# Local attention layers of a two-layer block: opening norm in pairs of chunks, rotary sums by accumulating transfers, a stated program slot

## The reference

```
h = layernorm(x) * (1 + cb) + sb
for i in range(6):
    h = attn_layer(shift_tokens(h), ...) + h        # 16 heads of 64, windows of 32
    h = ffn_layer(shift_tokens(h), ...) + h
attn_layer: q = l2norm(q) * qs;  k = l2norm(k) * ksc
            q = q * cos * scale + rotate_half(q) * sin * scale
            k = k * cos / scale + rotate_half(k) * sin / scale
            softmax of a window's q against its own and the previous window's k, times v, times Wo
```

## Time and profile before

| | |
|---|---|
| median of 3 runs | 4979.4 us (4970.4 to 4989.2) |
| the profiled execution | 4985.0 us, its span 4983.1 us |
| busy in the span | TensorE 81%, VectorE 74%, ScalarE 63%, GpSimd 22% |
| DMA | 336.8 MB, 68 GB/s on average |

### The profile page before, as it was taken

How to read it: one execution, slowest core, us unless ns; L and a number is a source line. 1 busy time by engine, 2 the same in 40 slices (tenths; PEclk the granted TensorE clock), 3 DMA queues, 4 the chain that set the end, 5 groups by cost and what they waited for, 6 DMA issues and landing times. The chain is left out here.

```text
span 4983.1 us, 174228 instructions
## 1 busy us (share of the span) xinstructions
PE 4053.0 (81%) x68188; PEld 2876.0 (58%) x68188; DVE 3701.7 (74%) x6683; ACT 3147.4 (63%) x8447; POOL 1095.9 (22%) x856
## 2 busy tenths in 40 slices
PE   7947888888888888888888888888888888886578
PEld 4725566665666666665666656666666666654234
DVE  4837777777777877777777777787777777774765
ACT  4715766666666666766666667667766667663233
POOL 0002222222222222222222222222222222220112
PEclk9959999999999999999999999999999999997688
DMA  0012222222222222222222222222222222220000
GB/s 26 1 58 82 72 76 73 75 91 78 70 77 71 82 85 78 76 74 74 88 82 77 74 76 80 87 78 78 74 74 90 83 78 73 75 75 24 0 7 11
DMA packets 126167, 336.76 MB, mean 68 GB/s; under 512 B 32592, under 2 KB 33744, under 8 KB 125264
## 3 DMA queue, kind: packets, MB, share of 16 engines
q1 hardware_dynamic: 125520, 326.63, 20.4%
HBM read 22.41 MB, written 2.10 MB: 5 GB/s over the span
## 5 line engine op out<-in xcount | busy, mean ns | idle before, releaser
L1172 ACT ACTIVATE loc_probs<-loc_pair,loc_ebias,loc_rnorm 128x64 f32<-128x64 f32 x3072 | 1200.6, 433 | 10.9 <-DVE loc_ebias L1332 7.8
L873 POOL TENSOR_TENSOR loc_ks<-loc_mcos,loc_swapped 128x1024 f32<-128x1024 f32 x192 | 452.1, 2354 | 1776.6 <-DVE loc_kr L1320 1375.0
L920 PE MATMUL loc_pair<-loc_hs,loc_wqk 128*128 128x256 f32 x3072 | 751.4, 388 | 47.5 <-issue 43.1
L873 POOL TENSOR_TENSOR loc_qr<-loc_mcos,loc_swapped 128x1024 f32<-128x1024 f32 x192 | 452.2, 2355 | 1270.6 <-DMA loc_swapped<-loc_msin 1204.6
L1172 ACT ACTIVATION_READ_ACCUMULATOR loc_probs<-loc_pair,loc_ebias,loc_rnorm 128x1 f32 x3072 | 719.6, 234 | 0.0
L920 PEld LDWEIGHTS loc_pair<-loc_hs,loc_wqk 128*128 128x128 f32 x3072 | 568.0, 192 | 151.9 <-issue 64.4
L1330 DVE TENSOR_REDUCE loc_mx<-loc_pair 128x8 f32<-128x512 f32 x384 | 264.5, 689 | 410.1 <-PE loc_pair L964 402.9
L1272 DVE SCALAR_TENSOR_TENSOR loc_mcos<-loc_pair,loc_scal,loc_tab 128x1024 f32<-128x1024 f32 x384 | 490.5, 1277 | 86.7 <-ACT loc_sq L1154 65.3
L1154 ACT ACTIVATE loc_sq<-loc_pair 128x1024 f32<-128x1024 f32 x384 | 396.9, 1034 | 204.2 <-PE loc_pair L920 204.2
L1281 DVE SCALAR_TENSOR_TENSOR loc_msin<-loc_pair,loc_scal,loc_tab 128x1024 f32<-128x1024 f32 x384 | 489.6, 1275 | 9.1 <-DMA loc_swapped<-loc_msin 8.9
L964 PE MATMUL loc_pair<-loc_kr,loc_qr 64*32 64x64 f32 x24576 | 322.9, 226 | 122.0 <-issue 121.4
(11 more groups left out here) (228 smaller groups left out, 7457.6 us busy)
## 6 DMA issues: line engine op xcount, KB each, us to landing
loc_swapped<-loc_msin SPq DMA_DIRECT2D x768, 256.0 KB, 2.6
loc_veven<-loc_vodd SPq DMA_DIRECT2D x768, 64.0 KB, 2.2
loc_veven<-loc_vodd SPq DMA_DIRECT2D x384, 128.0 KB, 2.3
loc_wqk<-wqk_dram SPq DMA_DIRECT2D x12, 512.0 KB, 4.6
loc_wv<-wv_dram SPq DMA_DIRECT2D x6, 512.0 KB, 4.1
loc_wo<-wo_dram SPq DMA_DIRECT2D x6, 512.0 KB, 4.5
x<-xT_dram SPq DMA_DIRECT2D x1, 2048.0 KB, 7.4
loc_tab<-tables_dram SPq DMA_DIRECT2D x1, 2048.0 KB, 7.6
```

The lines of the kernel that those rows point to most:

```text
L873: nc.gpsimd.tensor_tensor(dst, mcos[i % 2][:, :], swapped[:, :], ALU.add).then_inc(rope_add, 1)
L920: ins = nc.tensor.matmul(pairs[b][:, p // 2, (p % 2) * UNIT:(p % 2 + 1) * UNIT], wqk[:, k, w:w + P], hs[u.odd][:, :], start=True, stop=True)
L1172: ins = nc.scalar.activation(probs[x][:, p, hp, :], pairs[b][:, hp, p * 2 * WIN:(p + 1) * 2 * WIN], ACT.Exp, bias=ebias[x][:, k:k + 1], sc ...
```

## The change

- The opening norm has two `LayerNorm` objects with buffers and banks of their own and one set of semaphores. Each phase is issued for both chunks of a pair before the next phase; TensorE's and VectorE's waits on `normed_ready` and `out_ready` go by pairs. The waits for the constants and the mask copies stand behind the loop.
- `mcos` and `swapped` are gone; `msin` and `ks` are double. `rotate_cos` writes into `ks` or `qr`, waiting for readers of two units before. GpSimd issues two transfers that add `msin`, even and odd partitions exchanged, to it. `rotated` and SyncE's `halves_across` are gone. `rotate_sin` waits for the transfer of the product two before; `scale_keys` and `scores` wait for two transfers each (`landed`). The `swap_ready` semaphores start at 0.
- TensorE's pipelined loop states `head_slot` 208: its first instruction is placed at slot 208 of a block of 256 program slots.

```diff
-    def tensor_mean(self, pe, n, src, wide):
+    def tensor_mean(self, pe, n, src, wide, before=None):
-        pe.wait_ge(self.normed_ready, START + n)
+        pe.wait_ge(self.normed_ready, START + (n if before is None else before))
...
-        mcos = [sb(f"mcos{i}", [P, HALF_Q]) for i in range(2)]
-        msin, swapped = sb("msin", [P, HALF_Q]), sb("swapped", [P, HALF_Q])
-        qr, ks = [sb(f"qr{i}", [P, PAIRS, UNIT]) for i in range(2)], sb("ks", [P, PAIRS, UNIT])
+        msin = [sb(f"msin{i}", [P, HALF_Q]) for i in range(2)]
+        qr, ks = ([sb(f"{s}{i}", [P, PAIRS, UNIT]) for i in range(2)] for s in ("qr", "ks"))
...
+        def rotated_part(i, u):
+            g = 4 * (i % 2)
+            return (ks if i < 2 else qr)[u.odd][:, g:g + 4, :]
+
+        def landed(eng, i, n):
+            if not isinstance(n, int) or n >= 0:
+                eng.wait_ge(swap_ready[i], SWAP * n + SWAP)
...
-            with nc.Fori(FILL // 2, TOTAL // 2, engines=bass.OrderedEngineSet([eng.engine]), hint_back_edge=True) as i:
+            with nc.Fori(FILL // 2, TOTAL // 2, engines=bass.OrderedEngineSet([eng.engine]), hint_back_edge=True,
+                         head_slot={eng.engine: 208} if eng is nc.tensor else None) as i:
...
-            def halves_across(i, u):                                  # SyncE
-                after(sp, rot, u.n, 8, 2 * i + 2)
-                after(sp, rope_add, u.n, 4, i)
-                for half in range(2):
-                    sp.dma_start(swapped[1 - half:P:2, :], msin[half:P:2, :]).then_inc(swap_ready[i], 16)
...
-            def rotated(i, u):                                        # GpSimd
-                after(pool, swap_ready[i], u.n, SWAP, SWAP)
-                if i < 2:
-                    after(pool, kr_ready, u.n - 1, 2, 2)
-                else:
-                    after(pool, sim_ps, u.n - 2, 2, 2)
-                nc.gpsimd.tensor_tensor(dst, mcos[i % 2][:, :], swapped[:, :], ALU.add).then_inc(rope_add, 1)
+            def halves_across(i, u):                                  # GpSimd
+                after(pool, rot, u.n, 8, 2 * i + 2)
+                own_wait(pool, passed)
+                for half in range(2):
+                    there = rotated_part(i, u)[1 - half:P:2, :, :].rearrange("p g t -> p (g t)")
+                    pool.dma_start(there, msin[i % 2][half:P:2, :], accum_op=ALU.add).then_inc(swap_ready[i], 16)
...
             def step(at):                                             # GpSimd
-                rotated(0, at(2))
+                halves_across(0, at(2))
                 ffn_params(at(5))
-                rotated(1, at(2))
+                halves_across(1, at(2))
                 key_tail(at(2))
-                rotated(2, at(2))
+                halves_across(2, at(2))
                 tokens(at(1))
-                rotated(3, at(2))
+                halves_across(3, at(2))
...
-            pe.wait_ge(consts, START + 64)
-            pe.wait_ge(mask_ready, START + 2)
             with pe.Fori(0, BATCH) as b:
                 for c in range(2):
-                    ln.tensor(pe, b * 2 + c, x[:, bass.ds(b * SEQ + c * CH, CH)], bank(0), bank(1)[:, 0:4])
-            pe.wait_ge(ln.out_ready, START + NCH)
+                    lns[c].tensor_mean(pe, b * 2 + c, x[:, bass.ds(b * SEQ + c * CH, CH)], bank(c), b * 2)
+                for c in range(2):
+                    lns[c].tensor_var(pe, b * 2 + c, bank(2 + c)[:, 0:4])
+                for c in range(2):
+                    lns[c].tensor_spread(pe, b * 2 + c, bank(c))
+            pe.wait_ge(lns[0].out_ready, START + NCH)
+            pe.wait_ge(consts, START + 64)
+            pe.wait_ge(mask_ready, START + 2)
...
-                after(pe, rope_add, u.n, 4, 4)                        # scores
+                for i in (2, 3):
+                    landed(pe, i, u.n)
+                    own_wait(pe, passed)
...
-                after(dve, rope_add, u.n, 4, i - 1)                   # rotate_cos
+                if i < 2:
+                    after(dve, kr_ready, u.n - 2, 2, 2)
+                else:
+                    after(dve, sim_ps, u.n - 2, 2, 2)
...
-                after(dve, swap_ready[i - 1], u.n - (i == 0), SWAP, SWAP)      # rotate_sin
+                landed(dve, i - 2, u.n - (i < 2))
...
-                after(dve, rope_add, u.n, 4, 2)                       # scale_keys
+                for i in range(2):
+                    landed(dve, i, u.n)
```

More of the change, by code:

```diff
@@ L138 @@
 class LayerNorm:
+    EVENTS = tuple("ln_" + s for s in ("mean_ready", "centred_ready", "squares_ready", "var_ready", "rstd_ready", "spread_ready", "normed_ready", "out_ready", "links"))
     def __init__(self, nc, ctx, name, const, phase_sem, wide=None):
@@ L686, in local_layers @@
         flat = lambda i: pairs[i][:, :, :].rearrange("p a t -> p (a t)")
-        ln = LayerNorm(nc, ctx, "loc_ln", const, sem, (sq[:, 0, 0:CH], sq[:, 0, CH:], sq[:, 1, 0:CH]))
+        ln_sems = {s: sem(s) for s in LayerNorm.EVENTS}
+        lns = [LayerNorm(nc, ctx, f"loc_ln{c}", const, lambda s: ln_sems[s], wide)
+               for c, wide in enumerate(((sq[:, 0, 0:CH], sq[:, 0, CH:], sq[:, 1, 0:CH]), (sq[:, 1, CH:], sq[:, 3, 0:CH], sq[:, 3, CH:])))]
         mask32 = sq[:, 2, 0:BPS * 2 * WIN]
@@ L693, in local_layers @@
         w1_ready, w2_ready = sem("w1_ready"), sem("w2_ready")
-        hs_ready, qk_ps, sq_ready, rot, rope_add = sem("hs_ready"), sem("qk_ps"), sem("sq_ready"), sem("rot"), sem("rope_add")
-        swap_ready = [sem(f"swap_ready{i}") for i in range(4)]
+        hs_ready, qk_ps, sq_ready, rot = sem("hs_ready"), sem("qk_ps"), sem("sq_ready"), sem("rot")
+        swap_ready = [ctx.enter_context(nc.semaphore(f"loc_swap_ready{i}")) for i in range(4)]
         norm_ps, nT_ready, nT_ps, norm_read, rnorm_ready = sem("norm_ps"), sem("nT_ready"), sem("nT_ps"), sem("norm_read"), sem("rnorm_ready")
@@ L904, in _ @@
         def _(pe):
+            with pe.Fori(0, BATCH) as b:
+                for c in range(2):
+                    lns[c].tensor_mean(pe, b * 2 + c, x[:, bass.ds(b * SEQ + c * CH, CH)], bank(c), b * 2)
+                for c in range(2):
+                    lns[c].tensor_var(pe, b * 2 + c, bank(2 + c)[:, 0:4])
+                for c in range(2):
+                    lns[c].tensor_spread(pe, b * 2 + c, bank(c))
+            pe.wait_ge(lns[0].out_ready, START + NCH)
             pe.wait_ge(consts, START + 64)
             pe.wait_ge(mask_ready, START + 2)
-            with pe.Fori(0, BATCH) as b:
-                for c in range(2):
-                    ln.tensor(pe, b * 2 + c, x[:, bass.ds(b * SEQ + c * CH, CH)], bank(0), bank(1)[:, 0:4])
-            pe.wait_ge(ln.out_ready, START + NCH)
             def project(i, u, b):
@@ L1143, in _ @@
                 for c in range(2):
-                    n = b * 2 + c
-                    ln.scalar_squares(act, n)
+                    lns[c].scalar_squares(act, b * 2 + c)
+                for c in range(2):
                     at = b * SROW + c * CH
-                    ln.scalar_out(act, n, [(slice(0, DH), xaf[0:DH, bass.ds(at, CH)]), (slice(DH, P), xaf[DH:P, bass.ds(at + 1, CH)])], mods[:, 0:1])
+                    lns[c].scalar_out(act, b * 2 + c, [(slice(0, DH), xaf[0:DH, bass.ds(at, CH)]), (slice(DH, P), xaf[DH:P, bass.ds(at + 1, CH)])], mods[:, 0:1])
             def square(i, u, b):
@@ L1253, in _ @@
                 link.start(b)
[L1254 to L1255 removed]
+                dve.wait_ge(lns[0].normed_ready, START + 2 * b)
+                dve.wait_ge(lns[0].out_ready, START + 2 * b)
                 for k in range(3):
@@ L1260, in _ @@
                 for c in range(2):
-                    ln.vector(dve, b * 2 + c, x[:, bass.ds(b * SEQ + c * CH, CH)], bank(0), bank(1)[:, 0:4], mods[:, 1:2])
-            dve.wait_ge(ln.out_ready, START + NCH)
+                    lns[c].vector_centre(dve, b * 2 + c, x[:, bass.ds(b * SEQ + c * CH, CH)], bank(c))
+                for c in range(2):
+                    lns[c].vector_rstd(dve, b * 2 + c, bank(2 + c)[:, 0:4])
+                for c in range(2):
+                    lns[c].vector_normed(dve, b * 2 + c, bank(c), mods[:, 1:2], b * 2)
+            dve.wait_ge(consts, START + 64)
+            nc.vector.tensor_copy(mask[:, :, :].rearrange("p c j -> p (c j)"), mask32).then_inc(mask_ready, 1)
+            nc.vector.tensor_copy(ident16[:, :], ident[:, :]).then_inc(mask_ready, 1)
+            dve.wait_ge(mask_ready, START + 2)
+            dve.wait_ge(lns[0].out_ready, START + NCH)
             dve.sem_inc(xa_done, UNITS)
```

26 lines of the change are left out of this document (5 added, 21 removed).

## The result

Each row of a table below that has a ratio compares with runs of the kernel before on the same chip. The change took the median from 4978.1 us (4 runs) to 4730.1 us (4711.1 to 4739.6, 4 runs): ratio 0.9495, 95% interval 0.946 to 0.953. The forecast was 4800 us in a range from 4730 to 4955. Direction and mechanism were right, but the gain was 39% larger than forecast (248 against 179 us). The time lies at the very end of the range; as a share of the kernel before it lies just past it (0.9495, where 4730 of the 4979.4 that the prediction started from is 0.9499).

What follows compares the result with a forecast made beforehand. No engine was full: TensorE set the pace, held by VectorE, ScalarE and its own program. 4985 - 131 - 52 - 37 - 8 + 18 + 30 = 4805 us profiled, 4800 as timed median; range 4730 to 4955.

Steps and rivals of the forecast that it cites:

- Gain 1: Loop: without GpSimd's sums VectorE's `ebias` is short, `gated` frees its bank in time, TensorE's 130.7 us `act_out` wait goes.
- gain 2: Loop: layer norm root steps on VectorE are no longer stretched by a sum, so TensorE's 52.4 us `rstd` wait goes.
- what was not counted: Loop: TensorE's waits for ScalarE's `probs` (76.3 us) and `lsq` (61.1), said to end a chain no sum blocks.
- Costs of the rotary edit: Loop: +18 us for two waits per score group instead of one, +30 for descriptor writing and longer packets disturbing program fetches.
- Is a transfer early enough: Loop, before `scores(0)`: an accumulating pair takes 7.4 us (3.8 to 11.5) with 14.7 free, so it costs nothing.
- Opening and filling: Ahead of the loop: paired opening norm saves 37 us, filling steps without VectorE's waits for swapped halves and sums save 8.
- Slot: TensorE's loop head moved from slot 214 to 208: block bounds stay in the same groups, counted 0, +-9 us.
- Rival B: GpSimd blocks VectorE as long as before, now by writing descriptors; only opening and filling gain: 4953 us, chance 0.16.
- Rival C: Transfers pass 14.7 us and scores wait in each of 96 units; at 17 us 5021, slower than before; chance 0.12.
- Rival E: TensorE's program fetches suffer at their upper bound of 113 us: 4883 us, chance 0.04.
- Rival D: ScalarE's chain comes earlier too and half of `probs` and `lsq`, 69 us, goes: 4731 us, chance 0.08.

Runs made afterwards that it cites:

- e9: The kernel before, with each of GpSimd's rotary sums adding only 8 of the 1024 columns: 4722.8 us, ratio 0.951.
- e1: The change's rotary part with slot 208 stated, but with the opening norm of the kernel before: 4772.4 us, ratio 0.957.
- e11: The change, with SyncE's queue waiting again for the rotations but not for the landings of transfers: 4777.2 us, ratio 0.962.
- e2: The kernel before with only the new opening norm, its loop head kept at slot 214: 4941.0 us, ratio 0.989.
- e16: The change with the head of TensorE's loop at slot 192 in place of 208: 4769.9 us, ratio 0.960.
- e12: The change plus 8 plain transfers a unit issued by GpSimd, into a buffer that nothing reads: 4743.7 us, ratio 0.955.
- e3: The change without a stated slot, so the loop's head falls at 221: 4909.0 us, ratio 0.984.
- e8: The change, with SyncE's queue waiting again for both the rotations and the landings of transfers: 5275.9 us, ratio 1.061.
- e10: The kernel before, with each rotary sum replaced by two memsets that write the same destination and read nothing: 4756.1 us, ratio 0.957.

## Why the prediction came out as it did

- **Gain 1, gain 2 and what was not counted.** This is the step that failed, in size. It summed the two waits that it could explain, 131 + 52 = 183, as all that the sums cost. The runs have 250 for that step (e9 against before): 197 us of idle time and 52 of busy time. `act_out` and `rstd` went nearly as forecast: over the 44 periods they fell by 122 and 52. Left out were TensorE's busy time (52 us in e9, of which the clock can explain up to 41; 47 in the change, of which it can explain 14), because I took busy time as fixed, and some 10 us of `lsq`, which I had said no sum touches.
- **Costs of the rotary edit.** Forecast +18 and +30, measured 46 in the loop and 48 over the span (e1 against e9). That the number fits is luck as far as the runs tell: longer stalls at the block bounds are 51 us by themselves, with the slot moved and the transfers changed at once, and SyncE's freed queue, which I put at zero, is worth 24 to 63 (e11). What the two split waits cost alone was not measured.
- **Is a transfer early enough.** Right: 6.2 us a pair at most, against 7.4 taken and 14.7 free.
- **Opening and filling.** Forecast 37 and 8, measured 38.5 (e2) and 4 (e1), and 43.6 together in the change.
- **Slot.** "Count 0" for the step from the unstated 214 to 208 is not shown: no run has the changed kernel at 214. The time at the bounds rose from 7.0 us a period before to 7.7, 31 us over the loop, by the slot, the transfers or both, and 16 records more (e16) cost 40 us where I expected none. The stalls do stay in the same groups, as the text said. But it weighed that step alone. The other side of it, the place where the head would lie with the longer code and body and nothing stated, is 221; there the body ends three records behind a bound, and the price is 179 us (171 by the ratios). The prediction noted that the body of 2854 from 208 ends in the same block as before; it did not work out what another block costs.
- **Rival B** (GpSimd's descriptors stop VectorE), chance 0.16: refuted in after and in e12. **Rival C** (late transfers), 0.12: refuted, VectorE's sine products waited 2.2 us in all for a landing, its scaling of the keys 2.9 us in the loop, and TensorE's list has none. **Rival E** (fetches at the upper bound): the `issue` waits rose, at L1002 from 82.6 to 128.8 us and at L965 from 116.0 to 121.3, while others fell; all `issue` waits of TensorE together went from 6.2 to 6.6 us a period, 19 us over the loop, far from the 113 of the upper bound. **Rival D** (ScalarE's chain earlier), 0.08, stood at 4731, the time that came, but by another way: `probs` stayed (76.3 to 80.3), `lsq` lost 16, and 47 us came off TensorE's busy time.

## What to carry to other kernels

Where a short VectorE operation with two SBUF inputs is stretched, look for a GpSimd instruction that reads two SBUF inputs beside it; a shorter, a write-only, or a DMA-made one freed it here, and the gain can pass the sum of the named waits, since TensorE's clock and busy time can follow. In a long loop on TensorE, measure where the 256-record bounds fall: state the slot of the head and try several. 134 records between the last bound and the branch kept the time at the head under 0.9 us here, 118 did not (1.8). When a body grows, count its bounds again before anything else, and compare two versions of a kernel with the slot of each tried, or part of the difference is that of their slots.

## What was not expected of the hardware

- The place of a loop's head was worth from 4574 to 4909 us in one and the same kernel, more than the change itself; a bound cost up to 2.0 us, a late fetch at the branch 4.1.
- The accumulating transfer of 256 KB took 0.86 us (median) to issue on GpSimd and landed in 4.5 (3.2 to 7.4); the plain one from SyncE 0.53 and 2.7. With these transfers, the queue share of the DMA engines rose from 20.4% in one queue to 23.4% and 10.5% in two, for nearly the same bytes (336.8 and 336.6 MB). First the kernel before:

```profile
q1 hardware_dynamic: 125520, 326.63, 20.4%
```

Then the change:

```profile
q0 software_dynamic: 61440, 201.38, 23.4%
q1 hardware_dynamic: 64080, 125.25, 10.5%
```

- TensorE's time at the lower granted clock in the loop was 58 us in e9, 314 in e3 and 618 in e8, where its waits are longest, and its busy time per period 71.9, 73.7 and 77.2 us. Longer stalls are not all of it: e10 has 9.8 us of idle time a period and e9 9.5, and yet 119.5 us at the lower clock against 58.0, each in one profile.
